# Slots 1 to 5 of a retention and FFN kernel in another order, and projections in column halves

## The reference, cut to what matters

```
q, k = rotary(x @ Wq), rotary(x @ Wk)            # 4 heads of 64
v    = x @ Wv                                    # 4 heads of 128
o    = retention(q, k, v)      # decayed causal scores @ v, plus q @ state; state += k^T v
y    = rmsnorm(o) * gn_weight * silu(x @ Wg)
x1   = layernorm(x + y @ Wo)
out  = layernorm(x1 + (silu(x1 @ Wgate) * (x1 @ Wup)) @ Wdown)    # hidden size 768, integer weights
```

## Time and profile before

| | |
|---|---|
| median of 3 runs | 436.63 us (435.69 to 437.12) |
| the profiled execution's own time | 435.4 us |
| its span in the profile | 433.7 us |
| PE matmul busy | 421.2 us (97%) |
| DVE, ACT, POOL busy | 307.3, 259.8, 189.7 us |

### The profile page before, as it was taken

How to read it: one execution, slowest core, us unless ns; L and a number is a source line. 1 busy time by engine, 2 the same in 40 slices (tenths; PEclk the granted TensorE clock), 3 DMA queues, 4 the chain that set the end, 5 groups by cost and what they waited for, 6 DMA issues and landing times.

```text
span 433.7 us, 11989 instructions
## 1 busy us (share of the span) xinstructions
PE 421.2 (97%) x4096; PEld 391.5 (90%) x4096; DVE 307.3 (71%) x893; ACT 259.8 (60%) x801; POOL 189.7 (44%) x333
## 2 busy tenths in 40 slices
PE   8998999999999999999999999999999999999993
PEld 3786888999999999999999999999999999998993
DVE  4888565668767686766777766777777677877764
ACT  5577655567665675666565566566656656554541
POOL 2332243455443454444354444344543444444564
PEclk9999999999999999999999999999999999999999
DMA  7931010011100011110011111011110100100011
GB/s 231 382 138 51 0 50 2 26 39 38 38 21 24 34 39 39 38 36 12 24 36 36 36 36 36 0 36 36 36 36 13 38 2 14 38 14 15 14 38 39
DMA packets 16229, 19.63 MB, mean 45 GB/s; under 512 B 1472, under 2 KB 13760, under 8 KB 16192
## 3 DMA queue, kind: packets, MB, share of 16 engines
q1 hardware_dynamic: 16192, 19.14, 13.7%
HBM read 14.94 MB, written 4.19 MB: 44 GB/s over the span
## 4 chain that ended last, share of the span: by engine, by line
PE 92%; DVE 3%; POOL 1%; issue 1%; ACT 1%; DMA 1%; POOLq 0%; DVEq 0%; ACTq 0%
PE b_rows L447 32%; PE b_ffn L447 19%; PE b_rows L465 9%; PE b_rows L461 6%; PE b_head L621 6%; PE b_turn L655 3%; PE b_head L591 3%; PE b_head L583 3%; PE b_ffn L610 2%; PE b_turn L475 2%; PE b_state L640 2%; PE b_state L632 1%; DMA xT_raw<-in_xT 1%; PE b_head L587 1%; POOL h_lo L1568 1%
## 5 line engine op out<-in xcount | busy, mean ns | idle before, releaser
L1568 POOL TENSOR_TENSOR h_lo<-wf_int,h_hi 128x256 fp32r<-128x256 f32 x96 | 71.1, 740 | 98.4 <-ACT h_hi L984 97.7
L447 PE MATMUL b_ffn<-x1T_lo,wf_hi 128*128 128x256 f32 x384 | 92.1, 277 | 0.9 <-issue 0.9
L447 PE MATMUL b_ffn<-x1T_hi,wf_hi 128*128 128x256 f32 x384 | 92.6, 278 | 0.0
L447 PEld LDWEIGHTS b_ffn<-x1T_lo,wf_hi 128*128 128x128 f32 x384 | 72.2, 188 | 1.5 <-issue 1.1
L447 PEld LDWEIGHTS b_ffn<-x1T_hi,wf_hi 128*128 128x128 f32 x384 | 72.1, 188 | 0.6 <-DVE wf_int L1281 0.2
L952 ACT ACTIVATE sq<-b_head 128x128 f32<-128x128 f32 x124 | 34.4, 277 | 53.1 <-PE b_head L621 50.1
L984 ACT CAST h_hi<-wf_int 128x256 fp32r<-128x256 f32 x96 | 38.8, 404 | 45.5 <-DVE wf_int L1281 44.9
L1586 POOL TENSOR_TENSOR ve<-mv,eps 128x1 f32<-128x1 f32 x64 | 14.2, 222 | 112.4 <-DVE mv L1388 93.7
L1281 DVE TENSOR_TENSOR wf_int<-b_ffn,wf_int 128x256 f32<-128x256 f32 x96 | 40.3, 420 | 17.0 <-ACT wf_int L973 14.1
L1379 DVE TENSOR_TENSOR z<-b_rows,x_sb 128x256 f32<-128x256 f32 x32 | 13.6, 424 | 46.2 <-PE b_rows L447 46.1
L447 PE MATMUL b_rows<-wf_hi,h_hi 128*128 128x256 f32 x192 | 45.7, 278 | 0.3 <-POOL h_lo L1568 0.3
(11 more groups left out here) (157 smaller groups left out, 1212.8 us busy)
## 6 DMA issues: line engine op xcount, KB each, us to landing
xT_raw<-in_xT SPq DMA_DIRECT2D x16, 256.0 KB, 3.0
x_sb<-in_x SPq DMA_DIRECT2D x16, 256.0 KB, 2.8
out<-wf_int SPq DMA_DIRECT2D x32, 128.0 KB, 1.7
wf_int<-in_w_ffn SPq DMA_DIRECT2D x6, 384.0 KB, 6.5
wf_int<-in_w_proj SPq DMA_DIRECT2D x6, 256.0 KB, 4.7
rope_sb<-in_rope SPq DMA_DIRECT2D x4, 256.0 KB, 6.6
rope_q<-in_rope_by_row SPq DMA_DIRECT2D x2, 512.0 KB, 9.2
wo_raw<-in_w_o SPq DMA_DIRECT2D x1, 512.0 KB, 7.8
```

The source lines that it names most:

```text
L447: mm = pe.matmul(dst, a, b, start=(i == 0 and j == 0 and not begun), stop=(i == n - 1 and j == len(passes) - 1 and not more), skip_group_c ...
L1568: pool.tensor_tensor(h_lo[:, ring, hb], h_full[:, u], h_hi[:, ring, hb].bitcast(F32), ALU.subtract).then_inc(h_split[j], 1)
```

## The change

On PE, `project` halves the passes of slots 2 to 7: for qk the last 4 of 6 (c = 0, whole = 2), for v all six (c = 1, whole = 0), for g the last 3 from slot 5 on (c = 2, whole = 3). Slot 1, and g of slots 2 to 4, stay whole. In slots up to 4 `retain` goes ahead of `attention_out`. `sum_wide` leaves the end of slot 4 and stands behind the qk projection of slot 5, followed there by the v projection of slot 5, which before stood between two FFN blocks. ACT takes the squares at the end of slots 1 to 4 in place of the start of the next slot, and its flag sums and weight splits shift around them; DVE has `gated_output` ahead of the rotation in slots 3 to 5 and the rotation's last step behind `split_y`, and `tell_wide` at the start of slot 5; POOL has `rms_norm` ahead of `inv_std_1` up to slot 5.

```diff
-                for cols in (slice(0, 256), slice(256, 512)):
+                for c, cols in enumerate((slice(0, 256), slice(256, 512))):
...
-                        mm = pe.matmul(dst[:, cols], a, b[:, cols], start=False, stop=i == n - 1,
+                        mm = pe.matmul(dst[:, cols], a, b[:, cols], start=c == 0 and i == 0, stop=i == n - 1,
...
-                elif natural(s):
+                elif is_slot(s, 1) or c == 2 and natural(s) and s <= FFN_LAG:
                     mm = split_product(dst[:], stat, mov)
                 else:
-                    mm = projection_passes(dst, stat, mov, (None, 2, 3)[c])
+                    mm = projection_passes(dst, stat, mov, (2, 0, 3)[c] if natural(s) else (None, 2, 3)[c])
...
-                if natural(s):
+                if natural(s) and not is_slot(s, FFN_LAG + 1):
                     project(s, q, t, 1, v_done)
-                elif not gate_first(s, t):
+                elif not natural(s) and not gate_first(s, t):
...
             def to_outputs(s, q, t):
-                attention_out(s, q, t)
-                retain(s, q, t)
-                if is_slot(s, FFN_LAG):
-                    sum_wide()
+                if isinstance(s, int) and s <= FFN_LAG:
+                    retain(s, q, t)
+                    attention_out(s, q, t)
+                else:
+                    attention_out(s, q, t)
+                    retain(s, q, t)
...
             first_projection(s, s // TS, s % TS)
+            sum_wide()
+            project(s, s // TS, s % TS, 1, v_done)
             pe.wait_ge(wide_known, 2)
```

More of the change, by code:

```diff
@@ L1035, in steady_slot @@
                     turn_first_q()
[L1037 to L1041, removed]
+            def early_slot(s, q, t):
+                prev = (s - 1, *back(q, t, 1))
+                if s == 0:
                     copy_v(s, q, t)
@@ L1045, in slot @@
                     return
-                mean_squares(s - 1, *back(q, t, 1))
                 keep_qk(s, q, t)
[L1048 to L1051, removed]
+                keep_state(*prev)
+                if s == 4:
                     sum_low_ffn(2)
+                split_xT(s + 2, *back(q, t, -2))
+                copy_v(s, q, t)
+                if s == 1 or s == 2:
+                    split_ffn(s - 1)
@@ L1053, in slot @@
+                if s == 4:
+                    sum_low_ffn(5)
+                    keep_x1(s, q, t)
+            def first_ffn_slot(s, q, t):
+                keep_qk(s, q, t)
+                copy_v(s, q, t)
+                gate(s - 1, t - 1, 0)
+                split_xT(s + 2, *back(q, t, -2))
                 gate(s - 1, t - 1, 1)
                 split_h(s - 1, t - 1, 0)
[L1055 to L1072, removed]
+                keep_x1(s, q, t)
+                gate(s - 1, t - 1, 2)
+                split_h(s - 1, t - 1, 1)
+                split_x1T(s, q, t)
+                split_y(s, q, t)
+                split_h(s - 1, t - 1, 2)
+                gate_v(s, q, t)
+                gate(s, t, 0)
@@ new lines, in slot @@
+            def slot(s, q, t, ahead):
+                prev = (s - 1, *back(q, t, 1))
+                if not natural(s):
+                    steady_slot(s, q, t)
+                    return
+                if s <= FFN_LAG:
+                    early_slot(s, q, t)
+                    return
+                if s == FFN_LAG + 1:
+                    first_ffn_slot(s, q, t)
+                    return
+                mean_squares(*prev)
+                keep_qk(s, q, t)
+                keep_state(*prev)
+                gate(s - 1, t - 1, 1)
+                split_h(s - 1, t - 1, 0)
+                keep_x1(s, q, t)
+                split_h(s - 1, t - 1, 1)
+                split_xT(s + 2, *back(q, t, -2))
+                copy_v(s, q, t)
@@ L1441, in steady_slot @@
                 moments_1(s - 2, waited=True)
+            def early_slot(s, q, t):
+                prev = (s - 1, *back(q, t, 1))
+                if s < 3:
+                    norm_1(s, q, t)
+                    rotate_cos(s, q, t)
+                    rotate_sin(s, q, t)
+                    gated_output(*prev)
+                else:
+                    gated_output(*prev)
+                    norm_1(s, q, t)
+                    rotate_cos(s, q, t)
+                    rotate_sin(s, q, t)
+                if s < 3:
+                    rotate(s, q, t)
+                mask(s, q, t)
+                if s == 1:
+                    split_wo()
+                    split_ffn(0)
+                split_x1T(s, q, t)
+                split_y(s, q, t)
+                if s >= 3:
+                    rotate(s, q, t)
+                if s == 2 or s == 3:
+                    split_ffn(2 * s - 3)
+                    split_ffn(2 * s - 2)
+                if s == 4:
+                    split_ffn(5)
+                residual_1(s, q, t)
+                moments_1(s - 2)
+            def first_ffn_slot(s, q, t):
+                prev = (s - 1, *back(q, t, 1))
+                tell_wide()
+                gated_output(*prev)
+                norm_1(s, q, t)
+                rotate_cos(s, q, t)
+                hidden(s - 1, t - 1, 0)
+                rotate_sin(s, q, t)
+                hidden(s - 1, t - 1, 1)
+                mask(s, q, t)
+                hidden(s - 1, t - 1, 2)
+                split_x1T(s, q, t)
+                split_y(s, q, t)
+                rotate(s, q, t)
+                residual_1(s, q, t)
+                hidden(s, t, 0)
+                moments_1(s - 2, waited=True)
             def slot(s, q, t):
+                prev = (s - 1, *back(q, t, 1))
                 if not natural(s):
@@ L1461, in slot @@
                 mask(s, q, t)
-                if is_slot(s, 1):
-                    split_wo()
-                    split_ffn(0)
                 split_x1T(s, q, t)
                 split_y(s, q, t)
-                if is_slot(s, 2) or is_slot(s, 3):
-                    split_ffn(2 * s - 3)
-                    split_ffn(2 * s - 2)
                 residual_1(s, q, t)
[L1471 to L1477, removed]
+                hidden(s, t, 0)
+                moments_1(s - 2, waited=True)
             def drain():
@@ L1626, in slot @@
                 before = (s - 1, *back(q, t, 1))
-                inv_std_1(*before)
-                rms_norm(*before)
+                if s <= FFN_LAG + 1:
+                    rms_norm(*before)
+                    inv_std_1(*before)
+                else:
+                    inv_std_1(*before)
+                    rms_norm(*before)
                 split_h(s - 1, t - 1, 0)
```

39 lines of the change are left out of this document (19 added, 20 removed).

## The result

| | median us | runs | against before, in the same comparison |
|---|---|---|---|
| changed kernel, first comparison | 432.69 | 5 | 0.9934 (0.9917 to 0.9952); before 435.69 |
| second | 432.82 | 6 | 0.9952 (0.9938 to 0.9966); before 434.92 |
| third | 433.13 | 6 | 0.9947 (0.9930 to 0.9965); before 435.45 |

The forecast was 2.1 us, to 434.5, range 433.2 to 436.2. Two things add up: the kernel before ran at 434.9 to 435.7 in these comparisons and not at 436.63, and slots 2 to 7 of PE gained 2.80 us, not 2.16. The profiled execution of the changed kernel was 433.7 us, the longest of its five.

What follows compares the result with a forecast made beforehand. PE, busy for 97% of the span, was taken as the bound. Terms of -1.64 - 0.6 - 0.45 + 0.1 + 0.1 + 0.33 = -2.16, taken as -2.1 us, led from 436.63 to 434.5, range 433.2 to 436.2.

Steps and rivals of the forecast that it cites:

- term 1: Slot 4: PE's wait for y goes, with 0.18 us to spare; -1.64 us, bounds -1.64 and -1.1.
- term 2: Slots 2 to 4: retention ahead of attention_out covers the wait for yT_lo; 3 x -0.2 = -0.6 us, bounds 0 and -0.75.
- term 3: Slots 2 to 7: 69 passes of 512 become 138 of 256; -0.45 us, bounds +0.2 and -0.5.
- term 4: sum_wide leaves slot 4 and costs about 0.23 us between two projections of slot 5; +0.1 us (0 to +0.3).
- term 5: Slot 5: flag's load and branch behind v may outlast the time left; 0 to +0.4 us, taken as +0.1.
- term 6: Slot 5: without v between the FFN blocks, block 2 waits for hidden to read block 0; +0.33 us (+0.2 to +0.5).
- A: Slot 4: slower hand-overs only shorten the wait for y; gain 1.3 us, time 435.3; chance 0.14.
- B: ACT's squares and sums become the bound at sum_wide; gain 0.8 us, time 435.8, no measurable difference; chance 0.15.
- C: The branch in slot 5 waits for code, 0.9 us or 3.9 in all; slower, 438.4 us; chance 0.07.
- D: The halving does nothing or costs up to 0.2 us; time 435.0 to 435.2; chance 0.64 together with the forecast.

Runs made afterwards that it cites:

- the last three runs: Changed kernel with more 512-column passes halved: every one, all but the first of v in slots 8 on, or all but its first two; 435.89, 436.25, 431.99 us.
- all halves: Changed kernel with every 512-column projection pass halved, in all slots; 435.89 us, 1.0009 against the kernel before.

## Why the prediction was right or wrong

- *Slot 4's wait, term 1.* Right: -1.64, and each step of the chain within 0.05. Two of the orders were taken back singly, and the wait returned each time: with the Wo product first it is 1.23, with y behind the rotation 2.2. The orders of POOL and ACT were not.
- *Retention first, term 2.* Mis-sized: -0.6, measured -0.77. From g's end to `turn_qk` (in slot 4 with the flag's sum taken out) it was 2.54 and is 2.27, 2.31 and 2.27 in slots 2 to 4. I took 0.89 for the retention, from a row where other small matmuls follow it, and added 0.08 for the change of kind. Ahead of the Wo product it is 0.81 (35.53 to 36.34), and with the 0.08 to 0.09 that the second pass behind it comes later, the two together are the 0.89. The bound of -0.75 was too tight by the same mistake.
- *Halving, term 3.* Right: -0.45, measured -0.47 in slots. The cycles that the Trainium skill gives (TensorE: Matmul & The Clock Gate, Back-to-back issue gap), by which it would cost 0.17, do not hold in this stream. The other bound, a pace of 0.118, was worth keeping: the runs show that pace elsewhere, the halves of slots 2 to 7 escaped it, and no row said beforehand that they would.
- *The sum's place, term 4.* Right: +0.1, measured 1.59 for the sum and v (48.40 to 49.99) against 1.36 for v alone, 0.23, less the 0.14 before.
- *The branch, term 5.* 0 instead of +0.1: the first weight load stood at 49.88, 0.11 ahead of its pass as in any stream. Uncovered, load and branch take 0.7 (48.93 to 49.61).
- *The hidden block, term 6.* +0.28 (0.18 of waiting and 0.10 in the second pass), forecast +0.33:

```profile
51.69 0.28 PE L447 MATMUL b_ffn<-x1T_lo,wf_hi 128*128 128x256 f32 x1
51.99 0.39 PE L447 MATMUL b_ffn<-x1T_hi,wf_hi 128*128 128x256 f32 x1
52.21 0.28 PE L447 MATMUL b_ffn<-x1T_lo,wf_hi 128*128 128x256 f32 x1
```

- *A step that was missing: -0.24.* The prediction put what slot 5 could gain from a wait at nothing, since it looked only at waits that the profile named after an engine. Before, PE's scores of slot 5 started 0.33 behind the FFN block, with 0.17 called "issue":

```profile
54.14 1.11 DVE L1367 SCALAR_TENSOR_TENSOR y<-b_head,rms,g_sb 128x128 f32<-128x128 f32 x4
55.47 0.72 PE L587 MATMUL b_head<-qkT 64*128 64x128 f32 x8 [0.17 <-issue]
```

It was a second wait for y: from the start of y on DVE to the scores it is 1.33, as in slot 4 (1.36); the same 1.33 in the second trace of before and in the kernel with the halving alone. After, y is done 3 us ahead of the scores, and they start 0.09 behind the block. With `sum_wide` between slots 4 and 5, where y stands behind the rotation and the first hidden block, it is done 1.2 us ahead and they start at 0.09 too: what counts is when y is done, not that it comes first.

The measured terms are -1.64 - 0.77 - 0.47 + 0.09 + 0.28 - 0.24 = -2.75; the slots' lengths on PE (9.45, 9.66, 10.96, 12.82, 12.12, 13.47 before; 9.12, 9.38, 8.74, 13.02, 12.03, 13.39 after) give -2.80. The slots of the forecast were short of it in the same places: slot 4 at 8.9 came at 8.74, and slot 5 at 13.3 to 13.4 came at 13.02. So the mechanism was right, and the steps that failed in the sum are term 2 (0.17 too small), the wait in slot 5 that was put at nothing (0.24), and the branch (0.1): 0.5 of the 0.6 that were lacking. The other failed step is the base. The forecast and its range were laid from a median of three runs, 436.63, although the profiled execution was 435.4; five and more runs put the kernel before at 434.9 to 435.7. Of the 1.8 us between 434.5 and 432.69 the base is 0.9 and the gain the other 0.9; neither alone would have left the range.

The rivals: A did not happen, but it was near, as the margin is 0.13. B did not either: the last flag sum ended at 48.22 and PE came at 48.40; without the move it costs 1.5. C is refuted for this branch: the first weight load comes 0.2 us behind the register load, even uncovered. (PE's program ahead of the branch grew by 46 matmuls, not by 12: the halving of slots 2 to 5 counts too.) The "issue" of the drain, from which C took its 0.9, was no wait for code either but a third wait for y, of the same kind as the one in slot 5: that pass waits in `free_heads` for `y_ready`, y started at 397.70 and the pass at 399.04, 1.34 later, in the trace of before, and it was 1.34 again after.

```profile
397.70 1.13 DVE L1367 SCALAR_TENSOR_TENSOR y<-b_head,rms,g_sb 128x128 f32<-128x128 f32 x4 [0.96 <-POOL rms L1580]
399.04 0.36 PE L447 MATMUL b_ffn<-x1T_lo,wf_hi 128*128 128x256 f32 x1 [0.95 <-issue]
```

The Trainium skill's rule on taken branches (Runtime: NRT & Kernel Launch, Instruction fetch mechanics) thus did not show here; where the target lay, no run shows. D is refuted by the slots.

## What to carry to other kernels

Where one engine is the bound, write its arrival and the arrival of what it waits for as two sums from the same start; the smaller margin names the next wait, and a gap named "issue" may be a wait too if it keeps its distance to another engine's work. An order on one engine (retention first) pays only with the orders of the others that it feeds; the retention's place and y's place, each taken back singly, cost 4.6 and 4.1 us, more than the whole had gained. A wait can cost more than its length: read the granted clock behind it. Terms of 0.1% are measured in slots of the trace, not in medians.

## What the runs showed of the hardware that was not expected

A stream of 256-column passes with a weight load each has two paces, 0.1135 and 0.118 us, at a granted clock of 1.00 in both. In the steady slots of the last three runs the start decides: behind two 128-column transpositions the pace is the slow one with none or one 512-column pass ahead and the fast one with two; behind four transpositions it starts fast without any. It is not the whole rule. Five streams behind two transpositions with two whole passes ahead ran at 0.118 in the loop, two of them in the first trace of before (203.92 and 255.19), behind a stream that had itself turned slow midway. With all halves, the stream behind four transpositions in slot 4 (from 42.54) took 0.118, and the Wo passes of the changed kernel, always behind the eight matmuls of the retention, took 0.118 in slot 3 and 0.1135 in slots 2 and 4. What settles the pace stays open.

After PE had idled for 2.17 us the granted clock fell to half for 3.4 us; after 1.64 and 1.23 us it did not.
